# Attention scores of a two-layer decoder as 32-row products, four at once

## The reference

```python
Q = Q.reshape(B, S, 16, 8).transpose(0, 2, 1, 3)      # K and V alike
score = jnp.einsum('bhqd,bhkd->bhqk', Q, K) / jnp.sqrt(8)
attn_w = jax.nn.softmax(score, axis=-1)
out = jnp.einsum('bhqk,bhkd->bhqd', attn_w, V)
```

## Time and profile before

| | us |
|---|---|
| median of 3 runs | 421.82 (421.66 to 422.69) |
| the profiled execution | 420.76 |
| its span, first to last instruction | 419.0 |
| TensorE busy | 372.4 (89%) |
| VectorE busy | 284.1 (68%) |
| ScalarE busy | 224.7 (54%) |
| GpSimd busy | 54.3 (13%) |

### The profile page before, as it was taken

How to read it: one execution, slowest core, us unless ns; L and a number is a source line. 1 busy time by engine, 2 the same in 40 slices (tenths; PEclk the granted TensorE clock), 3 DMA queues, 4 the chain that set the end, 5 groups by cost and what they waited for, 6 DMA issues and landing times.

```text
span 419.0 us, 9114 instructions
## 1 busy us (share of the span) xinstructions
PE 372.4 (89%) x3274; PEld 328.2 (78%) x3274; DVE 284.1 (68%) x840; ACT 224.7 (54%) x526; POOL 54.3 (13%) x62
## 2 busy tenths in 40 slices
PE   4688898999889999699997999999997998979791
PEld 3576776887779898689986898978996877868691
DVE  6597889888965656732687346762569898864853
ACT  2155666665766564566447564676543866551231
POOL 7700004900000000000000000000003000111124
PEclk9699999999999999899999999999999999999997
DMA  5756410214250000200010000011012022552221
GB/s 160 197 173 182 115 53 24 77 46 116 98 150 2 2 2 0 77 2 2 1 52 25 2 2 2 0 50 29 2 28 62 3 76 70 169 178 64 62 64 34
DMA packets 23644, 25.68 MB, mean 61 GB/s; under 512 B 3241, under 2 KB 18354, under 8 KB 23601
## 3 DMA queue, kind: packets, MB, share of 16 engines
q1 hardware_dynamic: 22128, 23.47, 19.3%
q0 software_dynamic: 512, 0.97, 0.7%
q10 hardware_dynamic: 960, 0.66, 0.6%
HBM read 18.35 MB, written 6.83 MB: 60 GB/s over the span
## 4 chain that ended last, share of the span: by engine, by line
PE 70%; DVE 19%; issue 5%; ACT 2%; DMA 2%; POOLq 0%; SPq 0%; POOL 0%; ACTq 0%; DVEq 0%
PE bank_D L851 13%; PE bank_C L737 10%; PE bank_D L709 9%; PE bank_A L720 7%; DVE negmax L1250 5%; PE bank_A L867 4%; PE bank_A L869 4%; PE bank_A L868 4%; PE bank_D L635 2%; PE bank_D L768 2%; PE bank_D L693 2%; PE bank_A L655 1%; PE bank_D L751 1%; PE bank_A L1586 1%; DVE q_sp L1245 1%
## 5 line engine op out<-in xcount | busy, mean ns | idle before, releaser
L1250 DVE TENSOR_REDUCE negmax<-bank_D 128x2 f32<-128x512 f32 x192 | 127.8, 685 | 38.3 <-PE bank_D L709 37.6
L997 ACT ACTIVATE expo<-bank_A 128x512 f32<-128x512 f32 x192 | 109.7, 596 | 47.7 <-PE bank_A L720 45.9
L709 PE MATMUL bank_D<-k_head,q_sp 128*128 128x256 f32 x384 | 89.0, 317 | 6.4 <-DVE negmax L1250 3.1
L720 PE MATMUL bank_A<-q_sp,k_head 128*128 128x256 f32 x384 | 81.4, 296 | 4.1 <-DVE q_sp L1245 3.9
L1033 ACT ACTIVATE hidden<-bank_A,b 128x256 f32<-128x256 f32 x128 | 53.7, 471 | 54.2 <-PE bank_A L869 54.2
L709 PEld LDWEIGHTS bank_D<-k_head,q_sp 128*128 128x128 f32 x384 | 60.3, 196 | 18.5 <-issue 8.9
L851 PE MATMUL bank_D<-mix_w,hidden 128*128 128x128 f32 x512 | 67.9, 276 | 0.9 <-DVE qk_lo L1125 0.9
L720 PEld LDWEIGHTS bank_A<-q_sp,k_head 128*128 128x128 f32 x384 | 59.6, 191 | 6.6 <-DVE q_sp L1245 5.5
L851 PEld LDWEIGHTS bank_D<-mix_w,hidden 128*128 128x128 f32 x512 | 62.6, 192 | 2.2 <-issue 2.1
L737 PE MATMUL bank_C<-expo,v_aug 128*32 128x256 f32 x768 | 46.4, 382 | 0.6 <-ACT expo L997 0.3
L1309 DVE SCALAR_TENSOR_TENSOR y_mixture<-bank_D,g_w,y_mixture 128x128 f32<-128x128 f32 x64 | 22.3, 348 | 30.3 <-PE bank_D L851 26.2
(11 more groups left out here) (188 smaller groups left out, 513.5 us busy)
## 6 DMA issues: line engine op xcount, KB each, us to landing
mix_w<-in_mix_w SPq DMA_DIRECT2D x24, 256.0 KB, 3.7
k_head<-k_scratch SPq DMA_DIRECT2D x92, 48.0 KB
k_scratch<-qk_hi SPq DMA_DIRECT2D x24, 128.0 KB, 2.4
w_last<-in_mix_w SPq DMA_DIRECT2D x8, 256.0 KB, 5.5
k_scratch<-qk_lo SPq DMA_DIRECT2D x12, 128.0 KB, 2.3
proj_w<-in_proj SPq DMA_DIRECT2D x1, 640.0 KB, 5.4
xe_scratch<-empty_row SPq DMA_DIRECT2D x1, 520.0 KB, 4.7
expo<-xe_scratch SPq DMA_DIRECT2D x2, 260.0 KB, 3.0
```

Source lines behind the costliest of these rows:

```text
L709: last = mm(where(seq, b, ("max", k))[:, qt * SEQ:(qt + 1) * SEQ], q_sps[SET[seq, b]][:, k // 4, qt * P:(qt + 1) * P], k_heads[SET[seq, b] ...
L720: last = mm(where(seq, b, ("exp", h))[:, kt * SEQ:(kt + 1) * SEQ], k_heads[SET[seq, b]][:, t, g, kt * P:(kt + 1) * P], q_sps[SET[seq, b]][ ...
L997: activate(expo[:, exp_slot(seq, b, h), :], where(seq, b, ("exp", h))[:], ACT.Exp, scale=float(HD) ** -0.5).then_inc(free(seq, b, ("exp", ...
L1250: V.tensor_reduce(negmaxes[SET[seq, b]][:, s // 4, :, 32 * (s % 4)], where(seq, b, ("max", s))[:].rearrange("p (q n) -> p q n", q=QT), AX. ...
```

## The change

- `k_head` loses its second axis: it is 128 x 4 x 256, with the keys of head h in partitions 32 (h % 4) to 32 (h % 4) + 31 of column group h // 4. The zero padding is gone, and `clear_keys` clears a quarter of the bytes.
- Each score product takes only the 32 partitions of its head, from `q_sp` and from `k_head`.
- The scores leave the attention programs. `scores(tick)` is run at the head of every tick, before all programs. On TensorE it works in even ticks: two heads by query and two heads by key, in the order first half of both by query, first half of both by key, second half of both by query, second half of both by key. Waits for the banks stand ahead of the first half of each kind. The bank turns follow that order: two D turns and two A turns at once.
- On ScalarE and VectorE `scores(tick)` handles one head a tick, as before, but ahead of all other work of the tick.
- `EXP_AT` goes from 8 to 10, so the four heads of a tick lie in four different groups of 32 partitions; values and all that follows come two steps later. Starts move to even ticks: `(3, CROSS0)` from 121 to 122, `(0, CROSS1)` from 140 to 142, `(3, CROSS1)` from 204 to 208, the four mixtures from 83, 107, 131, 156 to 85, 109, 133, 159.

```diff
-EXP_AT = 8
-VALUES_AT = 17
-BACK_AT, CTX_AT, OUT_AT, ROOT_AT, NORM_AT, TURN_AT = 26, 28, 30, 31, 32, 34
+EXP_AT = 10
+VALUES_AT = 19
+BACK_AT, CTX_AT, OUT_AT, ROOT_AT, NORM_AT, TURN_AT = 28, 30, 32, 33, 34, 36
...
+def score_pairs(tick):
+
+    by_query, by_key = [], []
+    for seq, b, at in ATTENTION:
+        s = tick - at
+        if s % 2 == 0 and 0 <= s < HEADS:
+            by_query += [(seq, b, s), (seq, b, s + 1)]
+        if s % 2 == 0 and 0 <= s - EXP_AT < HEADS:
+            by_key += [(seq, b, s - EXP_AT), (seq, b, s - EXP_AT + 1)]
+    return by_query, by_key
...
+        scores(tick)
         live = [program for program in live if next(program, live) is None]
...
+    def scores(tick):
+        by_query, by_key = score_pairs(tick)
+        for seq, b, h in by_query:
+            turn(seq, b, ("max", h), "D")
+        for seq, b, h in by_key:
+            turn(seq, b, ("exp", h), "A")
...
-        k_heads = sets("k_head", [P, GROUPS, 4, SEQ], f32r)
+        k_heads = sets("k_head", [P, GROUPS, SEQ], f32r)
...
+                def score_by_query(seq, b, h, qt):
+                    r, t = rows_of(h), h // 4
+                    return mm(where(seq, b, ("max", h))[:, qt * SEQ:(qt + 1) * SEQ],
+                              q_sps[SET[seq, b]][r, t, qt * P:(qt + 1) * P],
+                              k_heads[SET[seq, b]][r, t, :], start=True, stop=True)
...
+                def scores(tick):
+
+                    by_query, by_key = score_pairs(tick)
+                    for one in by_query:
+                        wait_by_query(*one)
+                    for one in by_query:
+                        score_by_query(*one, 0)
+                    for one in by_key:
+                        wait_by_key(*one)
+                    for one in by_key:
+                        score_by_key(*one, 0)
+                    for seq, b, h in by_query:
+                        score_by_query(seq, b, h, 1).then_inc(full(seq, b, ("max", h)), 1)
+                    for seq, b, h in by_key:
+                        score_by_key(seq, b, h, 1).then_inc(full(seq, b, ("exp", h)), 1)
...
-                        if 0 <= s < HEADS:
-                            score_by_query(seq, b, s)
-                        if 0 <= s - EXP_AT < HEADS:
-                            score_by_key(seq, b, s - EXP_AT)
```

More of the change, by code:

```diff
@@ L110, in beginnings, with heads_at, by_the_clock @@
     return sorted(starts)
-def by_the_clock(attention, mixture, causal, routing):
+def score_pairs(tick):
[7 more added lines that the diff above has]
+    return by_query, by_key
+def heads_at(tick, start):
+    return [(seq, b, tick - at - start) for seq, b, at in ATTENTION if 0 <= tick - at - start < HEADS]
+def by_the_clock(attention, mixture, causal, routing, scores):
     stages = {SELF0: attention, CROSS0: attention, CROSS1: attention, MIX0: mixture,
@@ L220, in routing @@
             yield
-    by_the_clock(attention, mixture, causal, routing)
+    by_the_clock(attention, mixture, causal, routing, scores)
     return turns
@@ L482, in place_heads @@
                     eng.dma_start(
-                        k_heads[SET[seq, b]][r, 2 * half:2 * half + 2, g, :].bitcast(f32),
+                        k_heads[SET[seq, b]][r, 2 * half:2 * half + 2, :].bitcast(f32),
                         k_dram[SET[seq, b]][h].rearrange("t k j n -> (k j) t n")
@@ L703, in score_by_query @@
                         pe.wait_ge(k_head_ready[seq][0], 64 * (MHA[b] + 1))
-                    if k == 8:
+                    if h == 8:
                         wait_drained(pe, seq, b, "sq1")
                         pe.wait_ge(k_head_ready[seq][1], 64 * (MHA[b] + 1))
-                    wait_free(pe, seq, b, ("max", k))
-                    for qt in range(QT):
-                        last = mm(where(seq, b, ("max", k))[:, qt * SEQ:(qt + 1) * SEQ],
-                                  q_sps[SET[seq, b]][:, k // 4, qt * P:(qt + 1) * P],
-                                  k_heads[SET[seq, b]][:, k // 4, k % 4, :], start=True, stop=True)
@@ L712, in score_by_query @@
-                    last.then_inc(full(seq, b, ("max", k)), 1)
-                def score_by_key(seq, b, h):
-                    t, g = h // 4, h % 4
-                    if g == 0:
-                        wait_drained(pe, seq, b, ("shift", t))
-                    wait_free(pe, seq, b, ("exp", h))
-                    for kt in range(QT):
-                        last = mm(where(seq, b, ("exp", h))[:, kt * SEQ:(kt + 1) * SEQ],
-                                  k_heads[SET[seq, b]][:, t, g, kt * P:(kt + 1) * P],
-                                  q_sps[SET[seq, b]][:, t, :], start=True, stop=True)
-                    last.then_inc(full(seq, b, ("exp", h)), 1)
+                    wait_free(pe, seq, b, ("max", h))
@@ new lines, in score_by_key @@
+                def score_by_key(seq, b, h, kt):
+                    r, t = rows_of(h), h // 4
+                    return mm(where(seq, b, ("exp", h))[:, kt * SEQ:(kt + 1) * SEQ],
+                              k_heads[SET[seq, b]][r, t, kt * P:(kt + 1) * P],
+                              q_sps[SET[seq, b]][r, t, :], start=True, stop=True)
+                def scores(tick):
[12 more added lines that the diff above has]
+                        score_by_key(seq, b, h, 1).then_inc(full(seq, b, ("exp", h)), 1)
@@ L970, in _, with scores @@
                 bq = {CROSS0: col("bqx0"), CROSS1: 0.0}
+                def scores(tick):
+                    for seq, b, h in heads_at(tick, EXP_AT):
+                        wait_filled(act, seq, b, ("exp", h))
+                        if HEADS * ORDER[seq, b] + h >= ESLOTS:
+                            act.wait_ge(pair_done, (HEADS * ORDER[seq, b] + h - ESLOTS) // 8 + 1)
+                        activate(expo[:, exp_slot(seq, b, h), :],
+                                 where(seq, b, ("exp", h))[:], ACT.Exp, scale=float(HD) ** -0.5
+                                 ).then_inc(free(seq, b, ("exp", h)), 1)
                 def attention(seq, b):
@@ L1200, in _, with scores @@
                 bq = {CROSS0: col("bqx0"), CROSS1: 0.0}
+                def scores(tick):
+                    for seq, b, h in heads_at(tick, 0):
+                        wait_filled(dve, seq, b, ("max", h))
+                        V.tensor_reduce(negmaxes[SET[seq, b]][:, h // 4, :, 32 * (h % 4)],
+                                        where(seq, b, ("max", h))[:].rearrange(
+                                            "p (q n) -> p q n", q=QT),
+                                        AX.X, ALU.max, negate=True
+                                        ).then_inc(free(seq, b, ("max", h)), 1)
                 def attention(seq, b):
```

37 lines of the change are left out of this document (11 added, 26 removed).

## The result

The changed kernel took 487.45 us (median of 4, 480.64 to 497.61) against 422.09 us (median of 4, 421.66 to 422.69) for the kernel before: a ratio of 1.1415, with a 95% interval of 1.1357 to 1.1473. The forecast was 419.8, and its range ended at 431. The profiled execution took 491.14 us with a span of 489.3 (before 420.76 and 419.0), 70.3 us more. Runs more than 1.5% above the fastest of their kernel are left out of ratios, the profiled one among them, so the ratio gives a smaller loss (59.7 us of 422) than the quotient of the medians, 1.155, or the trace.

A forecast was written before the change was run, and what follows sets the result against it. TensorE was taken to bound the mixture stretch, and VectorE mostly the attention rounds. Terms -4.0 (mixtures), 0 (rounds) and +2.0 (starts and end) sum to -2.0 us, giving 419.8 us; range 408 to 431.

The forecast's parts named there:

- The block: Eight score products on TensorE, four at once: 0.87 us with switches for 1.18; full block saves 0.40, half loses 0.10.
- take turns: Rival: loads of row groups are not simultaneous, so only switches are added to score blocks; 449 us, chance 0.12.
- The attention rounds, 0: Stretches with attentions alone: new waits of pairs equal today's 2.6 us VectorE idling a round; 0 us, ends -21 and +22.
- the paired waits bite: Rival, even ticks of attention rounds: both banks and by-key wait ahead of second halves; +7.3 us, 427 us, chance 0.22.
- HOLD: Named with the experiments: VectorE and ScalarE take a pair's second head only in the odd tick, so its bank stays held.
- The mixture stretch, -4.0: Where mixtures run beside attentions: TensorE gains 5.6 us from blocks, less 1.6 for bank waits; -4.0 us, ends 2.6 and 9.0.
- the A pool: Banks for by-key scores and the mixture's up: TensorE stands where ScalarE also copies; 1.6 us off the mixture gain.
- The clock: Last sign of being wrong: a granted clock below full where TensorE now idles; no size, no chance.
- Starts, order and the end: New starts and last attention's end: +2.0 us, ends 0.5 and 4.5; maxima and exponents first in each tick: no separate gain.
- nothing more: Maxima and exponents first in each tick: banks return sooner, norm's chain at most 0.60 us later; no further effect.
- Edits at nothing: Clearing a quarter of k_head shortens GpSimd's start by some 2.6 us, key loads issue the same transfers; no effect on time.
- BOTH: Named with the experiments: TensorE waits for both banks of a pair, and those by key, before any second half runs.

The follow-up runs named there:

- e7: Kernel before plus unread product streams behind its work, on four row groups, then one: four take at most the 14.6 us of 120 full products; one falls to 0.50 clock.
- e6: e1 with one head by query and one by key in every tick instead of pairs: 425.91 us, 1.0037 of the kernel before.
- e1: The changed kernel with keys padded with zeros again, so score products run over 128 rows: 474.01 us, 1.1146 of the kernel before.
- e10: e1 with VectorE and ScalarE taking both heads of a pair in the even tick: 445.83 us, 1.0538 of the kernel before.
- e12: e1 with pairs only by query, and one head by key in each tick: 441.89 us, 1.046 of the kernel before.
- e4: The kernel before, in its own order, with only its score operands cut to 32 rows and keys unpadded: 513.62 us, 1.2061.
- e8: The changed kernel, 32 rows a product, with one head by query and one by key in every tick instead of pairs: 461.38 us, 1.0908 of the kernel before.
- e14: The changed kernel, 32 rows a product, with VectorE and ScalarE taking both heads in the even tick: 448.92 us, 1.053 of the kernel before.
- e5: The kernel before with only the new EXP_AT, VALUES_AT and starts: 427.54 us, 1.0083.
- e11: e6 with the constants and starts of the kernel before: 432.78 us, 1.0222 of the kernel before.
- e13: e1 with each head waiting for its own bank alone and both heads read in the even tick: 429.99 us, 1.0148 of the kernel before.
- e15: Kernel before plus unread product streams behind its work, on two, then three row groups, between 128-row streams: two and three groups keep full clock.

## Why the prediction was wrong

**The block: right.** Starts, halves and both switches came out as priced from the column tiles and L840: at full clock the second halves follow the first after 0.22 us, and the product in front and the one behind are some 0.21 us away. The loads did not take turns; e7 shows that outright. What was not priced is the block at half clock: there the second halves follow after 0.38 us (seven blocks).

**Where the time went.** The same maxima can be followed through the traces of e6, e1 and after as well. The forecast's terms stand beside what each stretch lost (us; each trace is of one execution, and the sums of the last three columns by the ratios are 1.6, 46.8 and 11.4):

| stretch, to which maximum | forecast | lost, after | starts and order (e6 less before) | pairs (e1 less e6) | 32 rows (after less e1) |
|---|---|---|---|---|---|
| start, to the second attention's first head | 0 | +4.0 | +0.5 | +4.6 | -1.1 |
| rounds, to the ninth head of the attention at tick 80 | 0 | +15.8 | -4.1 | +18.0 | +1.9 |
| mixtures, to the seventh head of the attention at 172 | -4.0 | +24.2 | -5.5 | +21.7 | +8.0 |
| rounds, to the ninth head of the last attention | 0 | +18.6 | +9.5 | +6.0 | +3.1 |
| tail, to the end of the span | +2.0 | +7.8 | +1.9 | +3.0 | +2.9 |
| all | -2.0 | +70.4 | +2.3 | +53.3 | +14.8 |

**The attention rounds, 0: wrong; this is the step that failed.** The bounds were -21 and +22, and my value was in the middle. The two stretches of rounds lost 34 us, 24 of them by the pairs. The mechanism was there, as the rival *the paired waits bite*: both banks ahead of either half, the second halves behind the wait by key. It was priced at 7.3 us, where the pairs cost 47 over the whole kernel. What was mis-sized is the number and the length of the exposed waits. I saw three places a round by query and priced only the one behind the values, with two by key, and counted as if the pair's second head were read right behind its first; with HOLD all other work of a tick lies between the two (28 us in e10, in all stretches). I also added each exposed wait up by itself, where in the ring TensorE's wait delays ScalarE's next exponent, which delays TensorE again; 62 to 66 us show this once, and no run tests it apart.

**The mixture stretch, -4.0: wrong sign, for the same reason.** It lost 24 us: 22 by the pairs and 8 by the 32 rows, less 5.5 that the new starts and order gave. I had counted TensorE's 5.6 us of gain and taken off 1.6 for the A pool, because ScalarE is idle 40% of this stretch. But a share of idle time says nothing about when a bank comes free. The second by key is read in the odd tick, behind the even tick's `hidden`, which itself waits for `up`. e1 keeps this order with 128 rows, and TensorE stands 23.4 us there, after 25.3; e12 puts two thirds of the pairs' cost on the A pool.

**The clock: no price, no chance.** It stood only in the last sentence, as something that would show if TensorE idled. It fell from 0.982 to 0.866, and idling doesn't explain that: in 30 to 115 us e1 leaves TensorE idle 14.7 us at a clock of 0.96, after 17.0 us at 0.84, and e4 has a lower clock still, 0.853, at 92% busy. In one burst of the values its cost can be read directly, over which the clock is 0.65:

```profile
59.29 2.90 PE L779 MATMUL bank_C<-expo,v_aug 128*32 128x256 f32 x32
```

2.90 us for the 32 products that took 1.93. Against e1, the 32 rows with their clock cost 11 us by the ratios (1.1415 less 1.1146, of 422), where the blocks alone should have gained. That price hangs on the rest of the order: it is 35.5 us without pairs (e8 against e6) and nothing with both heads read at once (e14 against e10). What part is the clock and what part exposed switches was not separated.

**Starts, order and the end.** In size nearly right: together 1.0037 (e6), the starts alone 1.0083 (e5), so the scores first are worth 1.9 us on the new starts; on the old ones they cost (e11), which "nothing more" didn't foresee. The place was off: e5 alone loses 8.8 us in the rounds behind the mixtures, where the last attention starts four ticks later and I had put 0.6, and makes part of it up before.

**Edits at nothing: right as far as seen.** Each of the two key tiles is cleared 2.56 us sooner, as priced (GpSimd's busy time falls from 54.3 to 49.1). No wait of TensorE for a key load is in the trace after. The second attention starts 4 us late, but so it does in e1 (5.1), which clears all the padding, and not in e6 (0.5): that too comes with the pairs.

The sum by the ratios, each step against the one before it (e5, e6, e1, after) and in us of 422: starts +3.5, scores first -1.9, pairs +46.8, 32 rows +11.4, together +59.7 (0.1415). My range was narrower than the bounds of its own middle term, -21 and +22; it followed the value chosen between them.

**Open:** why the clock falls with two or four groups side by side in these kernels and not in dense streams. The kernels have blocks of four to eight products between switches and other work; no run varied the length of a block. A kernel on 32 rows with neither BOTH nor HOLD was not run either. If rows cost nothing there, as in e14 against e10, it would lie near e13's 430 us and not beat the kernel before; that is an estimate.

## What to carry to other kernels

Before pairing work through a pool of three or four banks, follow each bank once round: who fills it, at which place of its own queue the reader takes it, and what stands behind the wait. A producer that takes two banks at once needs a reader that gives two back at once, and its own wait for each; an engine's idle share says nothing here. When products are cut to part of the array's rows, run the padded form of the same schedule beside it, and read the granted clock of both.

## What the runs showed of the hardware

- Row groups overlap fully: the four starts of a round lie within about 0.01 us, their loads overlap too, and 480 products of 32 rows by 256 columns in the time of 120 full ones, 4.0 times the rate (e7). The Trainium skill (TensorE: Matmul & The Clock Gate, Part 3) gives 3.07 for 512 columns; no run here has that size, and at 256 the measurement is above it.
- A switch of tiling cost 0.2 us each way in blocks of 8 (the trace after), as for the four products of L840. The Trainium skill (TensorEngine Tiling (Array Packing), Key Properties) names the drain; the trace agrees and gives its size.
- One row group alone, without a gap, lost the clock: 120 products in 21.5 us instead of 14.6, at first 0.12 us apart and then, at half clock, 0.213 (e7). Two, three and four groups in a dense stream kept it (e15, e7).
- Full products whose operand rows are three quarters zeros (the padded keys) kept full clock in the streams, except behind the single group, where they began at half clock and had the full one again after 7 us (e7, e15). In whole kernels the padded form had 0.959 (e1) and 0.975 (e6) where 32 rows had 0.866 (after) and 0.895 (e8): the padding was more than waste.
